# Loading tap weights by coefficient, and reordering the first two groups of a graph network kernel

## What is computed

```python
# layer 0
xc = transpose(x)                                  # features on partitions
h  = relu(bn(conv1d(xc, conv1_w, 0)))              # 1 tap
h  = bn(conv1d(h, conv2_w, pad=8))                 # 17 taps
x_conv = relu(h + xc)
s  = x @ w_se.T + b_se
A  = exp(-pairwise_distance(s))                    # then masked by adj
x_nmp = (A * adj) @ relu(x @ w_msg.T + b_msg)
y  = gru(input=[x_conv, x_nmp], hidden=x)          # gates r, z, n
x  = layernorm(x + y)
# layer 1
x  = layernorm(x + relu(((1 + eps) * x + adj @ x) @ W1 + b1) @ W2 + b2)
```

## Time and profile before

| | us |
|---|---|
| median of 3 runs | 372.45 |
| lowest and highest | 372.08, 373.14 |
| the profiled execution | 372.32 |
| its span, first to last instruction | 370.5 |
| PE busy | 360.1 (97%) |
| DVE busy | 315.2 (85%) |
| ACT busy | 230.0 (62%) |
| POOL busy | 154.9 (42%) |

### The profile page before, as it was taken

The page is one execution under the profiler, slowest core; times in us unless marked ns, Lnnn a source line. Parts: engine busy times, 40 slices in busy tenths (PEclk is TensorE's granted clock), DMA queues, the critical chain, the costliest instruction groups (busy, mean ns, idle before and its releaser), DMA issues.

```text
span 370.5 us, 6436 instructions
## 1 busy us (share of the span) xinstructions
PE 360.1 (97%) x2150; PEld 315.5 (85%) x2150; DVE 315.2 (85%) x707; ACT 230.0 (62%) x434; POOL 154.9 (42%) x158
## 2 busy tenths in 40 slices
PE   6999999999999999999999999999999999999993
PEld 3778889898889989899898998989888998988983
DVE  4999999999799969989699797989689895995685
ACT  3554775547766386666667467673875658464764
POOL 3121325264352833345342643618344463334362
PEclk9999999999999999999999999999999999999999
DMA  8400004301013011110013010120101201000002
...
DMA packets 8135, 19.39 MB, mean 52 GB/s; under 512 B 688, under 2 KB 5168, under 8 KB 7088
## 3 DMA queue, kind: packets, MB, share of 16 engines
...
...
## 4 chain that ended last, share of the span: by engine, by line
PE 83%; DVE 11%; DMA 2%; issue 1%; ACT 1%; POOL 0%; SPq 0%; POOLq 0%; DVEq 0%
PE back L1375 28%; PE conv L1375 22%; PE front L1500 8%; PE back L1500 6%; PE back L1596 6%; PE conv L1431 3%; PE back L1472 2%; DMA xv<-in_x_dram 2%; PE back L1552 2%; PE front L1492 1%; DVE adjT L1182 1%; PE conv L1472 1%; DVE amat L986 1%; DVE usum L999 1%; DVE xn L1097 1%
## 5 line engine op out<-in xcount | busy, mean ns | idle before, releaser
L1375 PE MATMUL conv<-sth,wh 128*128 128x256 f32 x207 | 61.5, 297 | 0.0
L1375 PE MATMUL conv<-sth,wl 128*128 128x256 f32 x207 | 59.0, 285 | 0.0
L1375 PE MATMUL conv<-stl,wh 128*128 128x256 f32 x207 | 59.0, 285 | 0.0
L554 POOL TENSOR_TENSOR rstd<-rstd,small 128x4 f32<-128x4 f32 (+1 forms) x34 | 39.1, 1151 | 44.1 <-DVE rstd L1079 43.5
L1375 PEld LDWEIGHTS conv<-sth,wh 128*128 128x128 f32 x207 | 39.1, 189 | 1.0
L559 POOL TENSOR_TENSOR xw<-xw,xv 128x512 f32<-128x512 f32 (+1 forms) x15 | 21.1, 1403 | 43.3 <-ACT xw L735 43.3
L1375 PEld LDWEIGHTS conv<-stl,wh 128*128 128x128 f32 x207 | 39.1, 189 | 0.0
L1375 PEld LDWEIGHTS conv<-sth,wl 128*128 128x128 f32 x207 | 39.1, 189 | 0.0
L665 ACT ACTIVATE sth<-sv 128x272 fp32r<-128x272 f32 (+1 forms) x33 | 17.3, 523 | 32.0 <-DVE sv L908 18.5
L752 ACT ACTIVATE tail<-tail,shift,rstd 128x128 f32<-128x128 f32 x60 | 24.1, 482 | 11.1 <-DVE shift L1133 11.1
L1500 PE MATMUL front<-amat,msg 128*128 128x256 f32 x128 | 29.2, 380 | 0.3 <-DVE amat L986 0.3
...
## 6 DMA issues: line engine op xcount, KB each, us to landing
...
xv<-in_x_dram SPq DMA_DIRECT2D x7, 512.0 KB, 3.2
...
tail<-in_conv_dram SPq DMA_DIRECT2D x1, 320.0 KB, 5.1
later_w<-in_later_dram SPq DMA_DIRECT2D x1, 320.0 KB, 7.3
```

The lines of the kernel that those rows point to most:

```text
L554: done(pool.tensor_tensor(rstd[:, k, v, q], rstd[:, k, v, q], minus_half[:, q], ALU.pow), RSTD[k])
L1375: ins = pe.matmul(bank, a, b, start=first and k == 0, stop=last and k == len(todo) - 1)
```

## The change

- **Weights by coefficient.** The host lays the 17 taps out so that each coefficient is contiguous, and the slots of `tail` are grouped in the same way. Coefficient 3 (4 taps) and 2 (5 taps) go first on ACT's queue, then `later_w`, then coefficient 1 (4 taps). Coefficient 0 (4 taps) goes on SP's queue, behind pair 1 of `x` and not ahead of it. There are three semaphores where there was one; DVE waits for coefficients 3 and 2 ahead of the first step, for 1 ahead of the second and for 0 ahead of the third. The wait of ACT for all taps is gone.
- **DVE's prologue.** The first step of `half` comes ahead of `x_low(0, 0, 0)` and `eps1`; the four `gbias` operations go to the end of the prologue, and ACT's wait for them to the end of its prologue. The zeroed slots and what `rouse` multiplies follow the new layout.
- **PE's prologue.** `plain_taps(0, HALF)` goes between the two `plain_conv1(1, ...)`.
- **Stage 1 on DVE.** `u_sum(1, 1)`, `pair1_sum(1)` and `x_low(2, ...)` go ahead of `mask(1, 1, 2..3)`.
- **The end on DVE.** `out_sum(g, 1, 1)` goes ahead of `out_shift(g, 0, WHOLE)`.

```diff
--- before.py
+++ after.py
@@ -81,7 +81,8 @@
                    + list(f["L1_gnn_b1"].reshape(2, P)) + [np.repeat(f["L1_gnn_eps"], P)]
                    + [np.full(P, s, np.float32) for s in SCALES], axis=1)
     o["first"] = np.concatenate([vec, f["L0_gnn_conv1_w"][:, :, 0].T], axis=1)
-    o["conv2"] = f["L0_gnn_conv2_w"].transpose(1, 2, 0)
+
+    o["conv2"] = f["L0_gnn_conv2_w"].transpose(1, 2, 0)[:, [k for j in (3, 2, 1, 0) for k in range((j - LEAD) % 4, TAPS, 4)]]
     ih = f["L0_gnn_w_ih"].reshape(3, P, 2, P).transpose(3, 2, 0, 1)
     hh = f["L0_gnn_w_hh"].reshape(3, P, P).transpose(2, 0, 1)
     o["gates"] = np.concatenate([hh, ih[:, 1], ih[:, 0]], axis=1)
@@ -188,8 +189,10 @@
 
 
         padded = tail[:, 0:4 * PLACES * P].rearrange("p (k o) -> p k o", o=P)
-        c2raw = padded[:, LEAD:LEAD + TAPS, :]
-        coef = [padded[:, j:4 * PLACES:4, :] for j in range(4)]
+        coef = [padded[:, j * PLACES:(j + 1) * PLACES, :] for j in range(4)]
+
+        c2raw = (coef[0][:, 1:5, :], coef[1][:, 1:5, :], coef[2], coef[3][:, 0:4, :])
+        C2_AT = (13, 9, 4, 0)
         gslots = gbuf[:, :, :, :].rearrange("p a h n -> p (a h n)").rearrange("p (k o) -> p k o", o=P)
         graw, gtaps = gslots[:, 0:9, :], gslots[:, 9:14, :]
         ataps = adjT[1][:, :, :, :].rearrange("p b r n -> p (b r n)").rearrange("p (k o) -> p k o", o=P)
@@ -308,7 +311,9 @@
         first_loaded = sem("first_loaded")
         x_pair0_loaded = sem("x_pair0_loaded")
         x_pair1_loaded = sem("x_pair1_loaded")
-        conv2_loaded = sem("conv2_loaded")
+        coef32_loaded = sem("coef32_loaded")
+        coef1_loaded = sem("coef1_loaded")
+        coef0_loaded = sem("coef0_loaded")
         gates_loaded = sem("gates_loaded")
         later_loaded = sem("later_loaded")
         mlp_loaded = sem("mlp_loaded")
@@ -487,8 +492,8 @@
             def prologue():
                 sp.dma_start(first_w[:, 0:NVEC + P], t["first"]).then_inc(first_loaded, 16)
                 sp.dma_start(xv[0][:, cols(0)], x_v[0, :, cols(0)]).then_inc(x_pair0_loaded, 16)
-                sp.dma_start(c2raw[:, 0:5, :], t["conv2"][:, 0:5, :]).then_inc(conv2_loaded, 16)
                 sp.dma_start(xv[0][:, cols(1)], x_v[0, :, cols(1)]).then_inc(x_pair1_loaded, 16)
+                sp.dma_start(c2raw[0], t["conv2"][:, C2_AT[0]:TAPS, :]).then_inc(coef0_loaded, 16)
                 load_x(1, 1)
                 sp.dma_start(ident, t["consts"]).then_inc(consts_loaded, 16)
                 sp.dma_start(later_w[:, W1_AT:], t["later"][:, W1_AT:]).then_inc(mlp_loaded, 16)
@@ -592,8 +597,8 @@
 
             def prologue():
                 pool.memset(minus_half[:, :], -0.5).then_inc(exponent_set, 1)
-                pool.memset(padded[:, 0:LEAD, :], 0.0).then_inc(ends_zeroed, 1)
-                pool.memset(padded[:, LEAD + TAPS:, :], 0.0).then_inc(ends_zeroed, 1)
+                pool.memset(padded[:, 0:PLACES + 1:PLACES, :], 0.0).then_inc(ends_zeroed, 1)
+                pool.memset(padded[:, 4 * PLACES - 1:, :], 0.0).then_inc(ends_zeroed, 1)
                 pool.memset(one[:, :], 1.0)
                 pool.memset(three[:, :], 3.0)
                 pool.memset(h1[:, :, :, :, :], 0.0).then_inc(pads_zeroed, 1)
@@ -764,10 +769,10 @@
                 act.activation(wh[:, k:k + NTAP[n], :], traw[n], ACT.Copy).then_inc(w_high, 1)
 
             def prologue():
-                act.dma_start(c2raw[:, 9:13, :], t["conv2"][:, 9:13, :]).then_inc(conv2_loaded, 16)
-                act.dma_start(c2raw[:, 13:TAPS, :], t["conv2"][:, 13:TAPS, :]).then_inc(conv2_loaded, 16)
-                act.dma_start(c2raw[:, 5:9, :], t["conv2"][:, 5:9, :]).then_inc(conv2_loaded, 16)
+                act.dma_start(c2raw[3], t["conv2"][:, C2_AT[3]:C2_AT[2], :]).then_inc(coef32_loaded, 16)
+                act.dma_start(c2raw[2], t["conv2"][:, C2_AT[2]:C2_AT[1], :]).then_inc(coef32_loaded, 16)
                 act.dma_start(later_w[:, 0:W1_AT], t["later"][:, 0:W1_AT]).then_inc(later_loaded, 16)
+                act.dma_start(c2raw[1], t["conv2"][:, C2_AT[1]:C2_AT[0], :]).then_inc(coef1_loaded, 16)
                 act.wait_ge(first_loaded, 16)
                 act.activation(wh[:, 0, :], c1raw, ACT.Copy).then_inc(w_high, 1)
                 act.wait_ge(x_pair0_loaded, 16)
@@ -778,7 +783,6 @@
                 h1_out(0, 1)
                 act.wait_ge(x_pair1_loaded, 16)
                 high(xh[0][:, cols(1)], xv[0][:, cols(1)], XH_READY)
-                act.wait_ge(conv2_loaded, 64)
                 x_high(1, 1)
                 for k in range(3):
                     msg_out(0, k)
@@ -791,7 +795,7 @@
                 h1_out(1, 0, True)
                 exps(0, 0)
                 exps(0, 1)
-                act.wait_ge(bn_ready, 3)
+                act.wait_ge(bn_ready, 2)
                 minus2_out(0)
                 exps(0, 2)
                 exps(0, 3)
@@ -812,6 +816,7 @@
                 tap_high(ZERO)
                 tap_high(HALF)
                 tap_high(PLUS2)
+                act.wait_ge(bn_ready, 3)
 
             def steady(s, u, front):
                 gb, gm, gf = s - 1, s, s + 1
@@ -1164,15 +1169,8 @@
                 dve.wait_ge(prep_chain, n[0])
                 dve.tensor_tensor(sc[:, :], vec[:, SCALE_AT:SCALE_AT + len(SCALES)],
                                   bn[:, 3:4].to_broadcast([P, len(SCALES)]), ALU.mult).then_inc(bn_ready, 1)
-                x_low(0, 0, 0)
-                link(dve.tensor_tensor(gbias[:, 0:3], vec[:, BIH:BIH + 3], vec[:, BHH:BHH + 3], ALU.add))
-                link(dve.tensor_scalar(gbias[:, 0:2], gbias[:, 0:2], 0.5, None, ALU.mult))
-                dve.tensor_scalar(gbias[:, 2:3], vec[:, BHH + 2:BHH + 3], 0.5, None, ALU.mult)
-                dve.tensor_copy(gbias[:, 3:4], vec[:, BIH + 2:BIH + 3]).then_inc(bn_ready, 1)
-                dve.tensor_scalar(eps1[:, :], vec[:, EPS1:EPS1 + 1], 1.0, None, ALU.add).then_inc(eps_ready, 1)
                 dve.wait_ge(ends_zeroed, 2)
-                dve.wait_ge(pads_zeroed, 2)
-                dve.wait_ge(conv2_loaded, 64)
+                dve.wait_ge(coef32_loaded, 32)
                 w0, w1, w2, w3 = coef
                 steps = [0]
 
@@ -1185,7 +1183,12 @@
                 even, odd = ataps[:, 10:15, :], utaps[:, 0:5, :]
                 dve.scalar_tensor_tensor(half, w3, 0.5, w2, ALU.mult, ALU.add).then_inc(tap_sums, 1)
                 steps[0] += 1
+                x_low(0, 0, 0)
+                dve.tensor_scalar(eps1[:, :], vec[:, EPS1:EPS1 + 1], 1.0, None, ALU.add).then_inc(eps_ready, 1)
+                dve.wait_ge(pads_zeroed, 2)
+                dve.wait_ge(coef1_loaded, 16)
                 taps_step(half, half, 0.5, w1)
+                dve.wait_ge(coef0_loaded, 16)
                 taps_step(half, half, 0.5, w0)
                 first_diffs(0)
                 half_stream(0)
@@ -1230,6 +1233,10 @@
                 w_low_part(wl[:, S_GATE:S_GATE + 9, :], graw, wh[:, S_GATE:S_GATE + 9, :], w_count("gates"))
                 xconv_low(0, 1)
                 x_low(0, 0, 1)
+                link(dve.tensor_tensor(gbias[:, 0:3], vec[:, BIH:BIH + 3], vec[:, BHH:BHH + 3], ALU.add))
+                link(dve.tensor_scalar(gbias[:, 0:2], gbias[:, 0:2], 0.5, None, ALU.mult))
+                dve.tensor_scalar(gbias[:, 2:3], vec[:, BHH + 2:BHH + 3], 0.5, None, ALU.mult)
+                dve.tensor_copy(gbias[:, 3:4], vec[:, BIH + 2:BIH + 3]).then_inc(bn_ready, 1)
 
 
 
@@ -1266,10 +1273,12 @@
                 w_low_part(w1l[:, :], w1raw, w1h[:, :], w_count("w1"))
                 h_low(0, 1)
                 tap_low(ZERO)
+                u_sum(1, 1)
+                pair1_sum(1)
+                x_low(2, 0, 0)
+                x_low(2, 0, 1)
                 mask(1, 1, 2)
                 mask(1, 1, 3)
-                u_sum(1, 1)
-                pair1_sum(1)
 
             def steady(s, u, front):
                 gb, gm, gf = s - 1, s, s + 1
@@ -1300,7 +1309,7 @@
                     h_low(gb, 1)
                     mask(gm, u, 2)
                     mask(gm, u, 3)
-                if front:
+                if front and not (isinstance(s, int) and s == 1):
                     x_low(gf, 1 - u, 0)
                     x_low(gf, 1 - u, 1)
                 pair2_add(gm)
@@ -1358,8 +1367,9 @@
                 out_shift(g - 1, 1)
                 out_stats(g, 0, WHOLE)
                 out_stats(g, 1, 0)
+                out_sum(g, 1, 1)
                 out_shift(g, 0, WHOLE)
-                out_stats(g, 1, 1)
+                out_norm_stats(g, 1, 1)
                 out_apply(g, 1, 0)
                 out_apply(g, 1, 1)
 
@@ -1603,8 +1613,8 @@
 
                 pe.wait_ge(ends_zeroed, 2)
                 for _ in range(5):
-                    pe.matmul(fb[1][:, 0:2 * P], padded[:, 0, :], padded[:, 0:2, :].rearrange("p k o -> p (k o)"),
-                              start=True, stop=True)
+                    pe.matmul(fb[1][:, 0:2 * P].rearrange("p (k o) -> p k o", o=P), padded[:, 0, :],
```

(3 more changed lines are left out.)

## The result

| | before | after |
|---|---|---|
| median, timed side by side | 372.23 (22 runs) | 372.97 (22 runs) |
| lowest and highest | 371.92, 373.28 | 371.89, 375.3 |
| the profiled execution, its span | 372.32, 370.5 | 372.84, 371.0 |
| granted clock in it | 0.999 | 0.999 |

The ratio is 1.0022 with an interval of 1.0012 to 1.0032: +0.7 us. That is "the same" by the bound of 0.3%, and close to the forecast (373.35 against 372.45, +0.24%). The size agrees in part by luck, though. Of the four terms of the sum only two (`gbias` and the end) came out as worked out, and a cost that the sum does not have at all, a lower clock of PE in part of the executions, is in the median.

What follows compares the result with a forecast made beforehand. The prediction took DVE's list to bound the kernel up to 63 us, PE being full behind it. Its terms +0.5 +0.53 -0.27 +0.14 summed to +0.9 us, taking the median from 372.45 to 373.35, range 372.1 to 374.2.

Steps and rivals of the forecast that it cites:

- The bound: Up to 63 us DVE's list is the clock; its idle time there appears at PE's 63.70 and stays.
- Term one: DVE's prologue: coefficient 1 lands at 9.5, second step of `half` at 9.6, `av` at 11.3 instead of 10.78: +0.5 us.
- Term two: Four `gbias` operations move from a place now idle into DVE's gapless stretch ahead of stage 1's messages: +0.53 us.
- The order of PE around HALF: PE's prologue: one 1-tap product behind HALF; `nmp` still waits for its mask, at 28.85: no cost of its own.
- The reasoning on PLUS1: PE reaches PLUS1 at 26.4, starting it 0.75 us late; at most 0.75 of an early-coefficient gain would get through.
- Term three: Stage 1: masks behind `xl`, done 1.2 us earlier; PE's wait at the 1-tap products, 72.72, goes: -0.27 us.
- three signs of being wrong: Second step without a wait; idle time elsewhere; PE's 1-tap products not 0.6 to 0.9 us later than 72.72.
- Term four: End on DVE: `shift` waits for item 2's sum, goes at 365.41, and sets SP's stores: +0.14 us; other end -0.3.
- Late coefficient 1: Rival, chance 0.27: coefficient 1 lands by bytes, 10.05 or worse; decides from 9.7; at 10.05 sum +1.45, 373.9 us.
- the early case: Rival, chance 0.18: coefficient 1 lands at 8.7 or before, `av` at 10.5, -0.3; sum +0.1, 372.55 us.
- `gbias` hidden: Rival, chance 0.10: slack on PE at 63.70 or a DVE pause between 42 and 63 hides 0.53; sum +0.4, 372.85.
- No effect on the messages: Rival taken for certain: `messages` not earlier on DVE whatever `later_w` does; costs nothing by itself, coefficient 1 pays the turn.

Runs made afterwards that it cites:

- the turn undone: Changed kernel with coefficient 1 ahead of `later_w` on ACT's queue: 371.63 us, ratio 0.9975 against the kernel before.
- the split load: Changed kernel with the 512 KB load of group 1's `x` on SP's queue sent as two of 256 KB: 372.23 us, ratio 1.0.
- both ahead of HALF: Changed kernel with both 1-tap products of group 1 ahead of HALF again: 372.55 us, ratio 1.0001.

## Why the prediction came out as it did, step by step

**The bound.** Right. A microsecond of DVE's idle time in the prologue goes through to the end at nearly its full size: the 1.37 us gained at `nmp` with the turn undone stayed 1.37 at the 1-tap products (71.52 against 72.89) and 1.3 of the span (369.7 against 371.0).

**Term one, coefficient 1 (+0.5).** Wrong in size, and the step is the landing "I take **9.5**". In the seven profiles with the changed order of loads and no split, the second step starts at 8.64, 8.86, 8.95, 9.09, 9.14, 9.30 and 9.69 and `av` 1.67 behind it: 10.77 on average, against 10.78 before. So the term is 0.0 on average, and between -0.5 and +0.6 in a single execution, against one profile of before, which is a single draw as well. I had taken a landing of one profile, 9.46, as if it were fixed. It is not: the same load behind the same list lands up to 1 us apart. Row for row is the likelier picture (the split load, one profile), and the fourth transfer did land near the place of the fourth before, 8.6 to 9.6 against 9.46; what was left out is that the whole set shifts from execution to execution. The mean start of the second step, 9.1, lies nearer to the early end (8.7 and 0.1) than to the 9.6.

**Term two, `gbias` (+0.53).** Right: +0.53 between 28.35 and 58.99 in the trace, and 0.59 by the run that puts them back. It shows first as a wait of 0.39 at 59.69, a place that I had not named, and only then at the `xn` of the forecast.

**The order of PE around HALF (0).** The reasoning on PLUS1 failed in its numbers. It had PLUS1 0.75 late, and it is 0.20 late (25.86 against 25.66); it had PE as a barrier for gains, and gains of 1.20 us pass. PE waited 2.38 us ahead of HALF, which I had not worked out. The term itself was 0.1 at most (both ahead of HALF). What I did not see is what the wait does to the clock. The rows for it were there: the 1-tap records filled PE's time up to HALF at 13.16, the earlier `later_w` moves the messages ahead of them 1.8 us forward (9.54 to 7.70 in the traces), and half of the 1-tap records, 0.9 us, is taken out. These sum to 2.7 us of hole, of which 2.38 show. I worked out only where DVE stood.

**Term three, the masks (-0.27).** The sign is right, the size at its place is not. Of the three signs of being wrong that the prediction named, the last one came: the 1-tap products start 0.17 us behind the 72.72 of before, not 0.6 to 0.9 (terms one and three each took about 0.3 of it). The bracket of 0.27 counts from the modelled end of the products ahead (70.50 + 1.95 = 72.45). Without a wait the next product starts ahead of that end: 71.19 + 1.95 = 73.14, and it starts at 72.89. So taking the wait away gives 0.27 + 0.25, the 0.53 of the table. Then 0.15 go again near 87 us, where the weight load of `back<-xh,wh` waits 0.24 to 0.27 us in all kernels with the moved masks and not before. From the first `nmp` product of that stage to the second 1-tap product it is 11.28 us before and 11.39 to 11.41 in the eight of them that I compared at this place. The profile names no cause ("issue"); it comes with the moved masks, also where they are moved alone, and I leave it open. Together -0.38, and -0.27 by the medians with the masks alone.

**Term four, the end (+0.14).** Right: 0.11 to 0.12 in the trace, 0.19 by the medians. The store follows `shift`, not the last statistics.

**The sum.** At full clock, with the mean of term one: 0.0 + 0.53 - 0.53 + 0.15 + 0.09 + 0.11 = +0.35. Measured at full clock: 372.67 against 372.23 (a plain median, since the clocks of those runs are not on record) and 372.62 against 372.19, so +0.4. The forecast had +0.9. The rest, 0.3 us of the median, is the clock. So term one was 0.5 us too high and the clock, 0.3 us, was missing; that the two nearly cancel is luck.

**The rivals.** Late coefficient 1 (a landing from 9.7 on): in none of the seven profiles; the latest landed at 9.6. Two of the seven lie in the forecast's 9.1 to 9.7, one (8.6) is as early as the early case, and the other four lie between; the average, 9.0, is nearer to the early 8.7 than to the 9.5. `gbias` hidden: refuted. No effect on the messages: they start at 7.70 on PE instead of 9.54, and DVE takes them up no earlier; this is so. But its price is not nothing, as I had written, since it is part of the hole ahead of HALF. With the turn undone I had given 372.1; it is 371.63, mainly because 1.20 us of the gain get through and not 0.75.
